# Reordering the fourth tile's tail in a four-layer transformer kernel: LN moments, h2 transposes, and half of a split moved to GpSimd

## The reference, cut to what matters

```python
def _layer(x, wqkv, qs, ksc, wo, lg, lb, w1, b1, w2, b2):
    h = shift_token(x)
    q, k, v = jnp.split(h @ wqkv, 3, axis=-1)      # 8 heads of 64
    q = l2norm(q) * qs; k = l2norm(k) * ksc
    q, k = rotary_xpos(q, k)
    o = local_attention(q, k, v)                   # window 128 and the one before
    x = x + o @ wo
    h = shift_token(x)                             # half of the features from the token before
    mu = h.mean(-1, keepdims=True); var = h.var(-1, keepdims=True)
    h = (h - mu) / jnp.sqrt(var + 1e-05) * lg + lb
    a, g = jnp.split(h @ w1 + b1, 2, axis=-1)
    x = x + (a * gelu(g)) @ w2 + b2
    return x

x = x + 0.5 * ffn(_layernorm(x))        # ffn: two such layers
x = x + attn(_layernorm(x))             # the memory
x = x + 0.5 * ffn(_layernorm(x))
```

## Time and profile before

| | us |
|---|---|
| median of three runs | 2497.58 |
| the profiled execution | 2497.31 |
| its span, first to last instruction | 2495.5 |
| PE busy | 2448.4 (98%) |
| DVE busy | 1981.1 (79%) |
| ACT busy | 1809.9 (73%) |
| POOL busy | 1562.9 (63%) |
| granted TensorE clock, mean | 0.999 |

### The profile page before, as it was taken

The page is one execution under the profiler, slowest core; times in us unless marked ns, Lnnn a source line. Parts: engine busy times, 40 slices in busy tenths (PEclk is TensorE's granted clock), DMA queues, the critical chain, the costliest instruction groups (busy, mean ns, idle before and its releaser), DMA issues. The chain is left out here.

```text
span 2495.5 us, 80211 instructions
## 1 busy us (share of the span) xinstructions
PE 2448.4 (98%) x29515; PEld 2190.9 (88%) x29515; DVE 1981.1 (79%) x6502; ACT 1809.9 (73%) x5232; POOL 1562.9 (63%) x1798
## 2 busy tenths in 40 slices
PE   8999999999999999999999999999999999999999
PEld 7889989999999889998766898999999988999998
DVE  7888888887877887777656888777777788888886
ACT  6778777777777777776554787777777777777776
POOL 6666667666666666665212676666666667666665
PEclk9999999999999999999999999999999999999999
DMA  3122011013000000005101000000003100000000
GB/s 128 38 88 74 26 58 55 28 37 111 17 4 4 3 3 29 4 15 204 36 19 36 4 3 3 4 4 4 4 4 126 37 3 20 20 20 21 21 21 29
DMA packets 80115, 85.04 MB, mean 34 GB/s; under 512 B 38938, under 2 KB 66030, under 8 KB 78574
## 3 DMA queue, kind: packets, MB, share of 16 engines
q1 hardware_dynamic: 78430, 78.45, 9.7%
q10 hardware_dynamic: 1296, 1.46, 0.2%
HBM read 49.53 MB, written 26.74 MB: 31 GB/s over the span
## 5 line engine op out<-in xcount | busy, mean ns | idle before, releaser
L676 POOL TENSOR_TENSOR pr<-pr,rden 128x384 f32<-128x384 f32 (+1 forms) x480 | 410.1, 871 | 273.0 <-DVE rden L1918 268.1
L888 ACT ACTIVATE pr<-pr,nb 128x192 f32<-128x192 f32 (+1 forms) x1024 | 438.0, 430 | 170.5 <-DVE nb L1909 170.5
L1213 PE MATMUL bank<-h2T,w 128*128 128x256 f32 x1344 | 386.0, 287 | 3.2 <-issue 0.9
L1214 PE MATMUL bank<-h2T,w 128*128 128x256 f32 x1344 | 376.9, 280 | 0.0
L1215 PE MATMUL bank<-h2T,w 128*128 128x256 f32 x1344 | 376.8, 280 | 0.0
L1909 DVE CUSTOM_DVE_ANT_0 pr<-bank,maskb,r 128x192 f32<-128x192 f32 (+1 forms) x1024 | 347.4, 393 | 24.9 <-PE bank L1285 23.3
L718 POOL TENSOR_TENSOR uTl<-t,uTh 128x256 fp32r<-128x256 f32 x288 | 218.0, 762 | 181.0 <-ACT uTh L988 147.9
L1213 PE MATMUL bank<-wqkv,hT 128*128 128x512 f32 x768 | 304.9, 397 | 1.8 <-DVE nb L1909 1.5
L1214 PE MATMUL bank<-wqkv,hT 128*128 128x512 f32 x768 | 302.5, 394 | 0.0
L1215 PE MATMUL bank<-wqkv,hT 128*128 128x512 f32 x768 | 300.1, 391 | 0.0
L2013 DVE SCALAR_TENSOR_TENSOR t<-bank,b,t 128x256 f32<-128x256 f32 (+1 forms) x384 | 184.4, 481 | 109.2 <-POOL uTl L718 47.4
(11 more groups left out here) (256 smaller groups left out, 7150.9 us busy)
## 6 DMA issues: line engine op xcount, KB each, us to landing
wqkv<-wqkv_split SPq DMA_DIRECT2D x18, 512.0 KB, 6.4
w<-w_split SPq DMA_DIRECT2D x3, 2816.0 KB, 10.8
Y<-in_x SPq DMA_DIRECT2D x8, 512.0 KB, 7.7
stt<-stt SPq DMA_DIRECT2D x256, 3.0 KB
out<-Y SPq DMA_DIRECT2D x8, 512.0 KB, 3.8
h<-out SPq DMA_DIRECT2D x7, 512.0 KB, 3.9
out<-h SPq DMA_DIRECT2D x7, 512.0 KB, 3.0
stt<-stt SPq DMA_DIRECT2D x192, 0.0 KB
```

Of the source, the lines that this page charges most:

```text
L676: e.tensor_tensor(probs(j, t), probs(j, t), rden[:, 2 * j:2 * j + 2].unsqueeze(2).to_broadcast([P, 2, w]), ALU.mult).then_inc(pn_done, 1 i ...
L888: last = e.activation(probs(j, t)[:, g, :], probs(j, t)[:, g, :], ACT.Exp, bias=nb[:, hd:hd + 1], scale=-1.0, accum_out=den[:, hd:hd + 1])
L1213: e.matmul(out, left[0], right[0], start=first, stop=False)
L1214: e.matmul(out, left[0], right[1], start=False, stop=False)
```

## The change

All in the fourth tile (t = 3) of each batch.

- DVE: `LN_moments(0)` right behind the second reciprocal; `WO` add and `halves` of tile 2 ahead of the `squares` of k; `LN_apply(0)` between `rotary` and `rotated` of q; the `squares` of q at the end, behind the add of W2; `H2T(0)` ahead of that add; `O` is no longer on DVE.
- POOL: the power for LN part 0 ahead of k's guard; a new `O_lower` between k's and q's work.
- PE: `H2T(0)` right behind the value product and ahead of the q and k transposes, into bank 3 (half 1 stays in bank 4), with no wait for the added O; W2's units are cut 9 and 7 around the value product, not 7 and 9; `WO` now stands alone between W2 and W1.
- ACT: `H2T(0)` ahead of `O`.
- `rotary` of q for a first tile waits for the squares of q.

```diff
+H2T_BANK = (3, 4)
 # POOL
+            def O_lower(L, b, t):
+
+                n = idx(L, b, t)
+                for i in pair:
+                    e.wait_ge(o_hi, at(o_hi, 2 * n + i + 1))
+                    e.tensor_tensor(oT[:, 1, 2 * i:2 * i + 2, :].rearrange("p a c -> p (a c)"), o_sum[:, 2 * P * i:2 * P * i + 2 * P],
+                                    oT[:, 0, 2 * i:2 * i + 2, :].rearrange("p a c -> p (a c)"), ALU.subtract).then_inc(o_lo, 1)
+                    if t == 3:
+                        LN(L, b, 0)
                     if ahead and t:
                         guard_k(*ahead)
                     if ahead:
                         A1_k(*ahead)
                     if t == 3:
-                        LN(L, b, 0)
+                        O_lower(L, b, t)
                     if ahead:
                         A1_q(*ahead)
 # ACT
                     if t == 3:
+                        H2T(L, b, 0)
                         O(L, b, t)
...
-                    if t == 3:
-                        H2T(L, b, 0)
 # PE
                 if half == 0:
                     e.wait_ge(pt_sb, at(pt_sb, 3 * idx(L, b, 3) + 3))
-                    e.wait_ge(o_added, at(o_added, sums(L, b, 3) + 2))
...
-                    cuts = (..., (0, 0, 7, UNITS))[t]
+                    cuts = (..., (0, 0, 9, UNITS))[t]
...
                         PV_first(L, b, t)
+                    if t == 3:
+                        H2T(L, b, 0)
                     if ahead and t:
                         A2(*ahead, 1)
                         A2(*ahead, 0)
...
                     if t == 3:
-                        H2T(L, b, 0)
                         WO(L, b, t)
 # DVE
-                if t == 1:
+                if t == 1 or t == 0 and i == 1:
                     e.wait_ge((sqk, sqq)[i], at((sqk, sqq)[i], m + 1))
...
                             R(L, b, t, j)
+                            if t == 3 and j == 1:
+                                LN_moments(L, b, 0)
                             if ahead and j == 2:
                                 rotary(*ahead, 0)
+                        if t == 3:
+                            if ahead:
+                                rotated(*ahead, 0)
+                            WO(L, b, t - 1)
+                            halves(L, b, t - 1)
+                            if ahead:
+                                squares(idx(*ahead), 0)
+                                rotary(*ahead, 1)
+                            LN_apply(L, b, 0)
+                            if ahead:
+                                rotated(*ahead, 1)
...
                     if t == 3:
-                        LN_apply(L, b, 0)
-                        O(L, b, t)
+                        H2T(L, b, 0)
                         if prev:
                             W2(*prev, t)
-                        H2T(L, b, 0)
+                        if ahead:
+                            squares(idx(*ahead), 1)
                         tile2_told(L, b)
                         WO(L, b, t)
                         halves(L, b, t)
```

More of the change, by code:

```diff
@@ L958, in H2T @@
                 lo = half * 2 * P
-                e.activation(columns(h2T, 0, lo, 2 * P), cut(bank[4][:, :], KT), ACT.Copy).then_inc(h2t_hi, 1)
+                e.activation(columns(h2T, 0, lo, 2 * P), cut(bank[H2T_BANK[half]][:, :], KT), ACT.Copy).then_inc(h2t_hi, 1)
             def table(func):
@@ L1380, in H2T @@
                         e.wait_ge(h2n_done, at(h2n_done, done + half + 2 * k + i + 1))
-                        mm = e.transpose(bank[4][:, (2 * k + i) * P:(2 * k + i + 1) * P],
+                        mm = e.transpose(bank[H2T_BANK[half]][:, (2 * k + i) * P:(2 * k + i + 1) * P],
                                          h2[:, 2 * half + i, k * P:(k + 1) * P], ident[:, :])
@@ L1478, in sequence @@
                     ahead2 = (L, b, t + 2) if t < NT - 2 else nxt and (*nxt, t - 2)
-                    cuts = ((5, 6, 11, 13, UNITS), (0, 0, 7, UNITS), (0, 0, 7, UNITS), (0, 0, 7, UNITS))[t]
+                    cuts = ((5, 6, 11, 13, UNITS), (0, 0, 7, UNITS), (0, 0, 7, UNITS), (0, 0, 9, UNITS))[t]
                     def fill(k):
@@ L1950, in H2T @@
                 e.tensor_tensor(h2T[:, 1, c:c + 1], bank[5][:, src:src + 1], h2T[:, 0, c:c + 1], ALU.subtract)
-                e.tensor_tensor(columns(h2T, 1, lo, 2 * P), cut(bank[4][:, :], KT), columns(h2T, 0, lo, 2 * P), ALU.subtract).then_inc(h2t_lo, 1)
+                e.tensor_tensor(columns(h2T, 1, lo, 2 * P), cut(bank[H2T_BANK[half]][:, :], KT), columns(h2T, 0, lo, 2 * P), ALU.subtract).then_inc(h2t_lo, 1)
             def no_neighbour():
@@ L2137, in sequence @@
                             R(L, b, t, j)
+                            if t == 3 and j == 1:
+                                LN_moments(L, b, 0)
                             if ahead and j == 2:
                                 rotary(*ahead, 0)
-                        if ahead:
+                        if t == 3:
[9 more added lines that the diff above has]
+                                rotated(*ahead, 1)
+                            if L == 0 and b == 0:
+                                beta()
+                        else:
                             rotated(*ahead, 0)
                             squares(idx(*ahead), 0)
[L2143 to L2147, removed]
+                            WO(L, b, t - 1)
                             squares(idx(*ahead), 1)
@@ L2150, in sequence @@
                             rotated(*ahead, 1)
-                        if L == 0 and b == 0 and t == 3:
-                            beta()
-                        if t < 3:
                             halves(L, b, t - 1)
```

## The result

The changed kernel takes **2502.99 us** (median of 9 runs, 2502.05 to 2505.07); the kernel before took 2497.53 beside it (9 runs, 2495.67 to 2498.61). The ratio is 1.0024, interval 1.0014 to 1.0035: slower by 0.24%, clear of noise, and at the edge of the 0.2% up to which the prediction called the time the same. The forecast was 2496.2; its range went to 2504. The profiled execution took 2504.01, with a span of 2502.2: 6.7 more than the span before.

A forecast was written before the change was run, and what follows sets the result against it. TensorE, busy 2448.4 of 2495.5 us, was taken as the bound, so only its waits could be won. Terms -0.6, -1.1 and +0.3 made -1.4: profiled 2497.31 to 2495.9, median 0.27 above, 2496.2 us; range 2487.5 to 2504.

The forecast's parts named there:

- LN moments "cost nothing": LN moments behind the second reciprocal take 0.53 on VectorE, covered by 0.64 idle ahead of the third reciprocal.
- Rival D: Early moments or k's later chain stop TensorE at P or k transposes; up to 0.3 a batch absorbed; chance 0.04.
- rival C: GpSimd is late at O's lower part, up to 0.49 a batch, moving WO: 2511.8 us, half 2504.7; chance 0.16.
- Late statistics: Second tile's statistics, behind weight loads in SP's queue in three batches: 0 to 0.5 us each, 0.3 in all.
- Both old stops go; the stop moves: Fourth tile: waits at q transposes and W1 (0.77 us a batch) vanish; new waits at WO, late h2; chance 0.54.
- WO at 1765.37 against 1765.38: WO's start, released by GpSimd's lower part of O, barely moves; TensorE, ready at 1765.07, waits 0.30 to 0.36.
- Chain of 7.3 from WO to the last h2 transpose: WO's last matmul through residual add, statistics, DMAs, moments, power and LN_apply to last h2 transpose: 7.3 us, unchanged.
- TensorE waits 0.36 at the last h2 transposes: Second half's h2 transposes wait 0.3 to 0.4 us for VectorE's L1995 in 29 batches.
- GpSimd's lower part 0.74: O's lower part takes 0.74 us on GpSimd against VectorE's 0.42, with no contention delay expected.
- Rival A: WO starts when TensorE is ready, at most 0.30 sooner in 29 batches: 2487.8 us; chance 0.22.
- The signs of being wrong: WO shifts over 0.13 us from P transposes, GpSimd's lower part exceeds 0.8, or WO-to-h2 span is not 7.3.
- The sum: Net -0.6 us over 29 batches, -1.1 in three with extra products, +0.3 for late statistics: together -1.4.

The follow-up runs named there:

- experiment 1: Changed kernel with only the addition of eps moved behind the fourth reciprocal, the joins staying early: 2498.42 us, ratio 1.0003 to the kernel before.
- experiment 3: Changed kernel with each addition of eps written as one instruction per column, in all three parts: 2503.53 us, ratio 1.0023 to the kernel before.
- experiment 4: Changed kernel with O's lower part back on VectorE, ahead of h2T's low part: 2493.69 us, ratio 0.9982 to the kernel before.
- experiment 6: Changed kernel with ScalarE's upper part of O ahead of its h2T copies: 2493.02 us, ratio 0.9984 to the kernel before.
- experiment 5: Changed kernel with three unused identity transposes added right ahead of the second half's h2 transposes: 2507.27 us, ratio 1.0039 to the kernel before.
- experiment 7: Changed kernel with eps addition behind the fourth reciprocal, O's lower part on VectorE before h2T's low part, ScalarE's upper O before h2T copies: 2481.63 us.

## Why the prediction was wrong, point by point

- **LN moments "cost nothing": the step that failed.** I summed 0.53 from the earlier trace rows, found 0.64 of idle time, and stopped. The sum was right for the durations of the old place. In the new place GpSimd's second product runs, and one of the five instructions waits for its end: 0.62 instead of 0.17. The third reciprocal comes 0.25 later, and 0.20 of it reaches the P transposes in 28 batches: 5.7 us. I had applied exactly this thought to the three GpSimd instructions that VectorE delays (the power, k's product, O's lower part), and not to VectorE's instructions that GpSimd delays. The trace of before held two cases, small ones: the 245 ns of batches 15 and 31, ending 0.03 behind a product. In the other 30 the addition stood beside GpSimd's power, which does not hold it, so its old duration told nothing of the new neighbour.
- **Rival D had the place and not the price.** It said that the early moments could stop TensorE at the P transposes, then gave the absorption of 0.3 at k to both its cases. Nothing behind PTE took the delay up: +5.67 ahead of it, and not less but 1.2 more behind. It was paid one for one. At 0.04 it was far too low. (C's 0.16 and D's 0.04 also make 0.20, not the 0.19 of the prediction.)
- **Late statistics, 0.3 in three batches:** +0.48, in batch 15 alone. VectorE idles 0.67 there for the move of statistics and the addition is not held (0.17); with the addition moved (experiment 1) the +0.46 stays. In batches 7 and 23 the joins were late too, but inside the time that the product holds the addition.
- **Batches 0, 1, 16 and 17** did not pay the 0.20, though their additions took 0.62 as well. Before, GpSimd's fourth product ended 0.44 to 0.52 ahead of the P transposes that take it there, and 0.06 to 0.16 ahead of them in the others: there was room for 0.25.
- **Both old stops go; the stop moves:** right. The q transposes have no wait; W1 stands 0.12 behind WO; WO waits for GpSimd, 11.7 in 32 places.
- **WO at 1765.37 against 1765.38:** off by 0.10 (6.15 against 6.05), the size of a term: `pick` and the h2 transposes took 0.71 and not 0.59, and ScalarE's copies and upper O came later by 0.10. The sum of it over the run is +1.6 at WO's start.
- **Chain of 7.3 from WO to the last h2 transpose:** right, 7.30 before and after. Experiments 3, 4 and 6 moved the chain by +0.10, -0.36 and -0.32 and moved the kernel with it.
- **TensorE waits 0.36 at the last h2 transposes:** there, 0.36 by the spacing of the four and by experiment 5, but not as a listed wait. I named a wait as the test, and by the view of waits I would have been wrong.
- **GpSimd's lower part 0.74, no contention (rival C):** right. It took 0.74 in every run that had it. **Rival A** did not come: on the way to WO no term was too long, and two were too short.
- **The signs of being wrong:** one of the three came. From the first P transpose to WO it is 7.22, before 6.95; from PTE, 6.15 and 6.07. Only the count that begins ahead of the P transposes shows the loss.
- **The range** to 2504 holds the 2502.99 by luck: its upper end was made for half of C, which did not come.
- **The sum.** Behind PTE the change brought +0.40 and +0.78, where -1.7 was worked out: 2.9 off, of which 1.8 at WO's last matmul and 0.8 behind the last h2 transposes, where I had set nothing. Batches 4 to 6 kept 0.26 to 0.29 each, where 0.36 was meant. With the P transposes' 5.7, less the 0.3 set for late statistics, that makes 8.2; the span came out 8.1 above the forecast's 2494.1 (2495.9 less 1.8).

The Trainium skill (SBUF — State Buffer, Who interferes with whom) says that VectorE's second pair of SBUF ports is shared with GpSimd, that a `tensor_scalar` can take it, and that the later instruction then waits until the first has ended. The runs agree for the products: 0.62 beside a product of 0.83, 0.30 beside one of 0.51, 0.15 beside none. They do not for GpSimd's power of eight: the addition began 0.28 behind its start, while it ran 1.67, and took 0.17. Why the one holds and the other does not, no run here shows. The prediction took from the Trainium skill (GPSIMD Engine Reference, Specifications) that GpSimd contends with VectorE instructions that have two SBUF inputs; the same line also names those in a 2-port mode, which the prediction left out, and it looked for the delay in one direction alone. The Trainium skill (VectorE: DVE Perf Modes, Mode 2×_2P) asks for an outermost non-unit dimension that is even, or odd and equal for source and destination. Four columns have it and were held; a single column has no non-unit dimension and was not held (experiment 3). That this mode is what makes the difference fits these two forms, and was tried with no other.

## What to carry to other kernels

When an instruction is moved into idle time, price it beside its new neighbours, not by its old duration, and in both directions: what it may delay on the engine that shares its ports, and what may hold it. Put what can be held behind the last instruction that another engine is waiting for, as experiment 1 does. Count from a point ahead of everything that was moved, or a stop in front of the first count stays unseen. And when a wait moves to the slower of two engines, look first at how late its input comes: putting O's upper part ahead of a copy that could wait gave as much (10.0) as taking the slower engine out (9.3), and with experiment 1's edit both together gave 21.4.

## What the runs showed of the hardware that was not expected

- A VectorE `tensor_scalar` of 4 fp32 values a partition, SBUF to SBUF, took 0.15 with GpSimd idle, 0.17 beside GpSimd's power of eight, and up to 0.63 beside a GpSimd `tensor_tensor` of 128x384, ending 0.02 to 0.03 behind it in 31 of 32 batches; with that product cut to 0.51 it took 0.30. `RECIPROCAL` and `BATCH_NORM_AGGREGATE` beside the same products were not held (`RECIPROCAL` 0.17 in experiment 3, with a product under way).
- The same addition as four instructions of one column took 0.34 in all in that place.
- A stop of TensorE need not appear among the waits of its matmuls. It lost 0.20 at each of 28 P transposes, and 0.36 at the late h2 transposes, with almost nothing listed for either. The waits of the weight loads had 5.4 of the first; the second was in no view of waits, only in the width of the group (1.02 against 0.65) and in added work that cost nothing.
- The step behind a stop is wider: from WO's first matmul to its second it is 0.19 with a stop ahead and 0.12 without (experiment 7).
